# Grouped attention layer: scores and exponentials passed on in halves of 512 columns, small remainders moved between VectorE and GpSimd

## The chip, the cores and the metric

One core of one Trainium2 chip runs the whole program. The metric is the device time of one execution in microseconds (us), the median of several runs. A TensorE instruction is called a matmul; VectorE is DVE in the rows, ScalarE is ACT, GpSimd is POOL, SyncE (which here only starts transfers) is SP, and PEld is TensorE's load of the stationary operand.

## The reference

Four cross-attention layers are applied one after the other to x (4 batches, 512 tokens, 256 channels) against one context (4 batches, 1024 keys, 512 channels). Layers 0, 2 and 3 have 16 heads of 64 channels:

```python
q, k, v = x @ Wq, ctx @ Wk, ctx @ Wv                  # 16 heads x 64
logits = q @ k.T * 64 ** -0.5 + col_bias              # -20 at a few keys, by mask
x = softmax(logits) @ v @ Wo + bo + x
```

Layer 1 is the grouped one: 16 query heads of 16 channels share 4 key and value heads, and x is normalized first:

```python
xn = rmsnorm(x) * norm_w
q, k, v = xn @ wq, ctx @ wk, ctx @ wv                 # 16 q heads, 4 kv heads, each of 16
x = x + softmax(q @ k.T / 4) @ v @ wo
```

## The kernel before

The work is cut into 112 steps p, numbered through all layers. A wide step (layers 0, 2, 3) is one batch with two heads; a group step (p = 32 to 47, `G0` to `G1 - 1`) is one batch with four query heads of one group. A step passes through *slots*: in slot s the scores and exponentials of step s are made, the maxima of step s + 1, the projections of q and k for step s + 2, and the normalization and output projection of step s - 1. Each engine has its own queue, and its order is written out by hand: `wide_slot`, `turned_slot` and `group_slot` say, separately for TensorE, ScalarE and VectorE, what comes after what, and GpSimd has one loop over the slots. Nothing is reordered by a planner. The engines meet only at semaphores, each a counter that a finishing instruction raises and another engine waits for.

High precision comes from splitting: an f32 value is kept as an f16 high part (made by ScalarE or GpSimd) and an f16 low part, the remainder (made by VectorE or GpSimd), and a product is three f16 matmuls (`products`). `weights_lo` and `wo_lo` make the remainders of the projection weights and of the output weights, `context_lo` that of the context, `split_x_lo` that of x. In the group layer the weights change every four steps, at the end of slots 32, 36, 40 and 44. The weights for the next set are read into one buffer, `w_raw`; the load of the set after it (SP queue, `load_w`) waits until the remainder is made.

The inner pipeline of a group slot, which the change touches, has sixteen units of i. In each, TensorE does two matmuls of maxima for the next step (`maxima`, into `ps_st`), then the scores of a unit j (`group_scores`): two matmuls of 64 rows each, one per half h, into the two banks of `ps_sm`, 512 columns a bank. ScalarE turns both banks into `pt` with one exponential of 1024 columns (`exponentials`, L1473). There is only one `ps_sm`, so the scores of unit j + 1 wait for the exponential of unit j. After every second unit TensorE multiplies four `pt` pieces with the values (`group_attend`, L1039). VectorE reduces each unit's maxima (L1893). Slot 47, the last of the group layer, is different: its maxima are only eight and four more units follow.

At the start (slots -2 and -1) the context is split: ScalarE makes the high parts `context_hi(0..7)`, the low parts are made by VectorE (0, 1, 3) and GpSimd (2, 4 to 7); the low part of x of batches 0 and 1 is made by GpSimd. TensorE's first projection of q (`project_q`) waits for the low part of x.

Of the kernel before, what the change touches and what calls it, by code (L numbers as in the profile page):

```python
# [53 lines left out]
def layer_of(p):  # L54
    return max(n for n in range(LAYERS) if p >= STARTS[n])


def grouped(p):
    return G0 <= p < G1
# [304 lines left out]
def build(nc, a, out):  # L364
    with ExitStack() as ctx:
# [3 lines left out]
        def sem(name):  # L369
            return ctx.enter_context(nc.semaphore(name))  # L370
# [78 lines left out]
        s_wo_l = sem("s_wo_l")  # L449
        s_init = sem("s_init")  # L450
# [24 lines left out]
        s_exp = sem("s_exp")  # L475
        s_acc = sem("s_acc")
# [189 lines left out]
        def _(pool):  # L666
# [31 lines left out]

            def normed_lo(b):
                pool.wait_ge(s_xn_h, b + 1)  # L700
                pool.wait_ge(s_q, queries(G0 - B + b + 1))
                G.tensor_tensor(of_batch(xl, b), sq[:], of_batch(xh, b), ALU.subtract).then_inc(s_xs, 1)
# [64 lines left out]
            for s in range(-2, N - 1):  # L767
                now, far, past = 0 <= s < N, 0 <= s + 2 < N, 0 <= s - 1
                summing = now and not grouped(s)
                if s == -2:  # L770
                    pool.wait_ge(s_ext_k, 1)
                    split_x_lo(0, 0)
                    context_lo(2)
                elif s == -1:
                    split_x_lo(0, 1)
                    for n in range(4, 8):
                        context_lo(n)
                splitting = s >= 0 and far and layer_of(s + 2) != GROUPED and s + 2 - STARTS[layer_of(s + 2)] < B
# [28 lines left out]
                if grouped(s + 1) and has_values(s + 1):  # L807
                    column_of_ones(s + 1, 0)
                    column_of_ones(s + 1, 1)
            last_slot()  # L810

        @block.tensor
        def _(pe):
# [201 lines left out]
            def group_scores(p, j):  # L1015

                kt, tile, r = j // 2, j % 2, p % 3
                if p == G0 and j == 0:
                    pe.wait_ge(s_max, units(p + 1))
                else:  # L1020
                    pe.wait_ge(s_exp, units(p) + j)
                if j < 2:
                    pe.wait_ge(s_tile, 2 * groups(p) + 1 + tile)
                for h in range(2):
                    d = slice(h * HD, (h + 1) * HD)
                    last = MM(ps_sm[:, h, :], k_h[d, r, kt * P:(kt + 1) * P], queries_in(p, tile)[d, :], start=True,  # L1026
                              stop=True)
                last.then_inc(s_st, 1)
# [352 lines left out]
        def _(act):  # L1381
# [75 lines left out]
            def exponentials(p, j):  # L1457
                n = units(p) + j
                act.wait_ge(s_st, n + 1)
# [12 lines left out]
                src = ps_sm[:] if grouped(p) else ps_st[:, j % 2]  # L1472
                A(pt[:, n % RING, :], src.rearrange("p h q -> p (h q)"), ACT.Exp).then_inc(s_exp, 1)  # L1473
# [323 lines left out]
        def _(dve):  # L1797
# [20 lines left out]

            def weights_lo(w):
                r = w % 2  # L1820
                dve.wait_ge(s_w_h, w + 1)
                if layer_of_set(w) == GROUPED:
# [14 lines left out]
            def wo_lo(w):  # L1837
                dve.wait_ge(s_wo_h, w + 1)
                split_lo(wo_l[:], wo_raw[:], WS, wo_h[:]).then_inc(s_wo_l, 1)
# [131 lines left out]
            for step in range(5):  # L1971
                token_rows(0, step)
            context_lo(1)
# [5 lines left out]
            def wide_slot(s):  # L1979
# [29 lines left out]
                if s < 0:  # L2009
                    if s == -1:  # L2010
                        dve.wait_ge(s_ctx_l[1], 1)
                        context_lo(3)
                        keys_lo(s + 2, 0)
                    queries_lo(s + 2)
                elif far:
                    keys_lo(s + 2, 1)
# [66 lines left out]
            def group_slot(s):  # L2083
# [11 lines left out]
                for i in range(16):  # L2095
# [36 lines left out]
                    if i == 5 and (s - 1) % B == 0:  # L2132
                        wo_lo(set_of(s - 1))
# [6 lines left out]
                if s % B == 0:  # L2140
                    weights_lo(set_of(s) + 1)
# [111 lines left out]
```

## Time and profile before

| | us |
|---|---|
| Median of 3 runs (3498.06 to 3499.04) | 3498.78 |
| The profiled execution, time | 3498.58 |
| The profiled execution, span from first to last instruction | 3496.4 |
| TensorE busy | 3364.5 (96%) |
| VectorE busy | 2350.3 (67%) |
| GpSimd busy | 2183.0 (62%) |
| ScalarE busy | 1766.3 (51%) |

The span is the stretch from the first to the last recorded instruction; 2.2 us of the execution's time lie around it. Busy time is the union of an engine's instructions, so that a busy TensorE may still wait between two matmuls whose recorded ends overlap. The mean granted clock of TensorE is 0.993 of full speed.

### The profile page before, as it was taken

To read this page: it belongs to the slowest core of one execution; us is meant where nothing else is said; L and a number is where in the kernel's file an instruction comes from. 1 tells how busy PE (TensorE), PEld (TensorE's weight loads), DVE (VectorE), ACT (ScalarE), POOL (GpSimd) and SP (SyncE) were. 2 spreads that over 40 slices of the span, in tenths; PEclk is the share of its full clock that TensorE was granted. 3 is DMA by queue.
4 is the path that set the end of the run, shared out by engine and by line. 5 is a ranking of instruction groups with operands and counts; after the bars stand their busy time and mean duration, and the time that the engine had idled before them with its cause. 6 is when DMAs were issued, how large, how long until landed. Compare 5 with 4: busy or idle time off the path is not lost.

```text
span 3496.4 us, 70163 instructions
## 1 busy us (share of the span) xinstructions
PE 3364.5 (96%) x27442; PEld 1544.6 (44%) x27442; DVE 2350.3 (67%) x4444; ACT 1766.3 (51%) x2230; POOL 2183.0 (62%) x1050
## 2 busy tenths in 40 slices
PE   6999999999997888889999999999999999999998
PEld 3444444444442322234444444444444444444443
DVE  5666666666656788856676666666666666666666
ACT  4444444444445677764444444444444444444444
POOL 4877777777650000028777777777787677767776
PEclk8999999999999999999999999999999999999999
DMA  4000000000000000000000000000000000000000
GB/s 145 10 10 10 1 10 10 9 3 9 6 10 11 8 12 17 17 1 10 10 1 10 10 10 1 10 10 9 3 10 10 1 10 10 10 1 10 3 1 25
DMA packets 50178, 42.10 MB, mean 12 GB/s; under 512 B 4928, under 2 KB 42176, under 8 KB 49856
## 3 DMA queue, kind: packets, MB, share of 16 engines
q1 hardware_dynamic: 49136, 37.08, 3.5%
q8 instruction: 225, 3.69, 0.4%
q14 instruction: 97, 0.79, 0.1%
q10 hardware_dynamic: 720, 0.53, 0.1%
HBM read 32.36 MB, written 2.10 MB: 10 GB/s over the span
## 4 chain that ended last, share of the span: by engine, by line
PE 90%; ACT 3%; DVE 3%; POOL 2%; issue 2%; DMA 0%; SPq 0%; ACTq 0%; POOLq 0%; DVEq 0%
PE ps_j L863 39%; PE ps_j L1052 19%; PE ps_st L1012 13%; PE ps_sm L946 6%; PE ps_st L997 3%; PE ps_j L1039 3%; ACT pt L1473 2%; PE ps_sm L1026 2%; POOL acc L719 2%; PE ps_j L1072 1%; PE ps_st L946 1%; PE ps_j L955 1%; PE ps_j L1088 0%; PE ps_j L1063 0%; DVE nmg L1893 0%
## 5 line engine op out<-in xcount | busy, mean ns | idle before, releaser
L719 POOL TENSOR_TENSOR acc<-acc,pt 128x1024 f32<-128x1024 f32 x570 | 1365.3, 2395 | 438.9 <-ACT pt L1473 384.8
L1473 ACT ACTIVATE pt<-ps_st 128x1024 f32<-128x1024 f32 x768 | 743.0, 1019 | 447.0 <-PE ps_st L1012 435.2
L1052 PE MATMUL ps_j<-pt,v 128*64 128x512 f32 x3040 | 694.2, 598 | 1.4 <-DVE q_l L1808 1.3
L1903 DVE CUSTOM_DVE_ANT_0 ps_sm<-ps_sm,bias_m,nmx 128x512 f32<-128x512 f32 x666 | 480.3, 757 | 272.6 <-PE ps_j L946 227.6
L863 PE MATMUL ps_j<-w_h,ctx_h 128*128 128x128 f16 x3072 | 532.6, 220 | 1.6 <-ACT rinv L1489 1.1
L863 PE MATMUL ps_j<-w_l,ctx_h 128*128 128x128 f16 x3072 | 531.5, 219 | 0.0
L863 PE MATMUL ps_j<-w_h,ctx_l 128*128 128x128 f16 x3072 | 531.4, 219 | 0.0
L1903 DVE CUSTOM_DVE_ANT_0 ps_sm<-ps_sm,bias_m 128x512 f32<-128x512 f32 x486 | 334.5, 706 | 197.1 <-PE ps_j L946 186.4
L740 POOL TENSOR_TENSOR o_un<-o_un,rinv 128x512 f32<-128x512 f32 x111 | 142.0, 1280 | 477.2 <-ACT rinv L1485 294.9
L1052 PEld LDWEIGHTS ps_j<-pt,v 128*64 128x64 f32 x3040 | 201.7, 136 | 407.6 <-issue 369.6
L1940 DVE RECIPROCAL rinv<-rinv 128x256 f32<-128x256 f32 x190 | 331.3, 1746 | 14.0 <-ACT rinv L1489 4.5
L1893 DVE TENSOR_REDUCE nmg<-ps_st 128x2 f32<-128x1024 f32 x248 | 296.0, 1217 | 45.7 <-PE ps_st L946 44.5
L863 PEld LDWEIGHTS ps_j<-w_h,ctx_h 128*128 128x128 f16 x3072 | 301.1, 98 | 54.9 <-issue 40.6
L863 PE MATMUL ps_j<-ctx_h,w_h 128*128 128x512 f16 x800 | 304.9, 381 | 15.5 <-DVE w_l L1808 13.1
L1473 ACT ACTIVATE pt<-ps_sm 128x1024 f32<-128x1024 f32 x256 | 261.6, 1022 | 104.7 <-PE ps_sm L1026 104.6
L946 PE MATMUL ps_sm<-k_h,q_h 64*128 64x512 f16 x1160 | 294.1, 381 | 14.3 <-DVE nmx L1903 11.6
L863 PEld LDWEIGHTS ps_j<-w_l,ctx_h 128*128 128x128 f16 x3072 | 301.4, 98 | 10.7
L863 PE MATMUL ps_j<-ctx_l,w_h 128*128 128x512 f16 x800 | 304.4, 381 | 0.0
L863 PE MATMUL ps_j<-ctx_h,w_l 128*128 128x512 f16 x800 | 304.2, 380 | 0.0
L863 PEld LDWEIGHTS ps_j<-w_h,ctx_l 128*128 128x128 f16 x3072 | 301.4, 98 | 0.0
L1433 ACT ACTIVATE k_h<-ps_j 128x512 f16<-128x512 f32 x192 | 114.6, 597 | 366.9 <-PE ps_j L863 366.9
L1012 PE MATMUL ps_st<-q_h,k_h 64*128 64x512 f16 x1488 | 282.4, 376 | 0.0
(186 smaller groups left out, 5483.0 us busy)
## 6 DMA issues: line engine op xcount, KB each, us to landing
w_raw<-wk SPq DMA_DIRECT2D x25, 256.0 KB, 2.7
pt<-ctx_t SPq DMA_DIRECT2D x6, 1024.0 KB, 7.8
w_raw<-wv SPq DMA_DIRECT2D x24, 256.0 KB, 3.7
wo_raw<-wo SPq DMA_DIRECT2D x28, 128.0 KB, 2.0
w_raw<-wq SPq DMA_DIRECT2D x24, 128.0 KB, 2.8
k_h<-k_l SPq DMA_DIRECT2D x72, 32.0 KB, 1.9
x<-x_t SPq DMA_DIRECT2D x4, 512.0 KB, 8.9
acc<-ctx_t SPq DMA_DIRECT2D x2, 1024.0 KB, 8.1
```

What stands on the lines that cost most here:

```text
L719: G.tensor_tensor(total, first, pt[:, n % RING, :], ALU.add).then_inc(s_acc, 1)
L740: G.tensor_tensor(o, o, rinv[:], ALU.mult).then_inc(s_o, 1)
L863: done = MM(dst, l, r, start=first and i == 0, stop=last and i == n - 1)
L946: last = MM(dst[h], queries_in(p, tile)[d, t * P:(t + 1) * P], k_h[d, r, half * HALF:(half + 1) * HALF], start=True, stop=True)
L997: MM(ps_st[:, j % 2, j // 2, :], ext_k[rows, buf, kt * P:(kt + 1) * P], ext_q[rows, p % 2, :], start=True, stop=False)
L1012: last = MM(ps_st[:, side, h, :], k[d, r, keys], q[d, r, :], start=False, stop=n == 2)
L1052: last = MM(dst[h * HD:(h + 1) * HD, :], values_of(p)[:, kt, h * HD:(h + 1) * HD], pt[:, (units(p) + kt) % RING, h * TQ:(h + 1) * TQ], sta ...
L1433: A(k_h[:, r, keys], bank(f"k{half}", p), ACT.Copy, scale=1 / WS).then_inc(s_k_h, 1)
L1473: A(pt[:, n % RING, :], src.rearrange("p h q -> p (h q)"), ACT.Exp).then_inc(s_exp, 1)
L1893: V.tensor_reduce(nmg[:, half, t, 2 * tile:2 * tile + 2], maxima_in(p, u), AX_X, ALU.max, negate=True).then_inc(s_max, 1)
L1903: last = V.tensor_tensor_reduce(out=src, in0=src, in1=bias_m[:, t, half * HALF:(half + 1) * HALF], scale=-1.0, scalar=nmx[:, 0, t, h:h + 1 ...
L1940: V.reciprocal(r, r).then_inc(s_rinv, 1)
```

## The change

In the group layer a unit's scores and exponential are passed on one bank at a time. `group_scores` waits for the first half of the previous exponential (`s_exp_first`), issues the matmul of half 0, then waits for the second half (`s_exp`), and issues the matmul of half 1; each of the two matmuls raises a semaphore of its own. `exponentials` becomes two activations of 512 columns, each of which waits for its own matmul.

The rests (the low parts) are dealt out differently. In the group layer GpSimd makes the low parts of the weights and of the output weights, at the end of slots 32, 36, 40 and 44; VectorE no longer does. [...] At the start VectorE makes the low part of x of batches 0 and 1, and GpSimd makes the context's low part 3, after waiting for the end of VectorE's mask preparation (`s_init`).

```diff
+            def weights_lo(w):                 # GpSimd
+                r = w % 2
+                pool.wait_ge(s_w_h, w + 1)
+                pool.wait_ge(s_w_l, w)
+                if layer_of_set(w) == GROUPED:
+                    cols = slice(WQ0, WQ0 + CQ * 2 * P)
+                    for c in range(CQ):
+                        cc = slice(WQ0 + c * 2 * P, WQ0 + (c + 1) * 2 * P)
+                        G.tensor_scalar(w_raw[:, cc], w_raw[:, cc], norm_w[:, c:c + 1], None, ALU.mult).then_inc(s_w_s, 1)
+                else:
+                    cols = slice(0, WCOLS)
+                    G.tensor_scalar(w_raw[:], w_raw[:], WS, None, ALU.mult).then_inc(s_w_s, CQ)
+                pool.wait_ge(s_w_s, CQ * (w - G0 // B))
+                G.tensor_tensor(w_l[:, r, cols], w_raw[:, cols], w_h[:, r, cols], ALU.subtract).then_inc(s_w_l, 1)
...
                 if s == -2:
-                    pool.wait_ge(s_ext_k, 1)
-                    split_x_lo(0, 0)
+                    pool.wait_ge(s_init, 1)
                     context_lo(2)
+                    context_lo(3)
                 elif s == -1:
-                    split_x_lo(0, 1)
                     for n in range(4, 8):
                         context_lo(n)
+                elif s == 0:
+                    pool.wait_ge(s_xs, 2)
...
+                if grouped(s) and s % B == 0:
+                    weights_lo(set_of(s) + 1)
+                    wo_lo(set_of(s))
...
-                    pe.wait_ge(s_exp, units(p) + j)
+                    pe.wait_ge(s_exp_first, units(p) - units(G0) + j)
...
-                    last = MM(ps_sm[:, h, :], k_h[d, r, kt * P:(kt + 1) * P], queries_in(p, tile)[d, :], start=True,
-                              stop=True)
-                last.then_inc(s_st, 1)
+                    if h and (p != G0 or j):
+                        pe.wait_ge(s_exp, units(p) + j)
+                    MM(ps_sm[:, h, :], k_h[d, r, kt * P:(kt + 1) * P], queries_in(p, tile)[d, :], start=True, stop=True
+                       ).then_inc(s_st if h else s_st_first, 1)
...
-                src = ps_sm[:] if grouped(p) else ps_st[:, j % 2]
-                A(pt[:, n % RING, :], src.rearrange("p h q -> p (h q)"), ACT.Exp).then_inc(s_exp, 1)
+                if grouped(p):
+                    A(pt[:, n % RING, 0:TQ], ps_sm[:, 0], ACT.Exp).then_inc(s_exp_first, 1)
+                    act.wait_ge(s_st, n + 1)
+                    A(pt[:, n % RING, TQ:2 * TQ], ps_sm[:, 1], ACT.Exp).then_inc(s_exp, 1)
+                    return
...
             split_x_lo(b):                     # VectorE, once after token_rows(0, ...), once in slot -1
+                dve.wait_ge(s_xs_h, b + 1)
+                V.tensor_tensor(of_batch(xl, b), of_batch(x32, b), of_batch(xh, b), ALU.subtract).then_inc(s_xs, 1)
...
                     if s == -1:
-                        dve.wait_ge(s_ctx_l[1], 1)
-                        context_lo(3)
+                        split_x_lo(1)
                         keys_lo(s + 2, 0)
...
-                    if i == 5 and (s - 1) % B == 0:
-                        wo_lo(set_of(s - 1))
...
-                if s % B == 0:
-                    weights_lo(set_of(s) + 1)
```

The instructions of TensorE keep their places; what differs are their waits. TensorE at the end of one unit of a group slot and in the next one (L946 are the maxima, L1026 the scores, L1039 the multiplication with the values), before:

```order
L1026 MATMUL ps_sm<-q_l,k_h 128x512 [waits s_tile,s_exp]
L1026 MATMUL ps_sm<-q_l,k_h 128x512
L946 MATMUL ps_st<-k_h,q_h 128x512 [waits s_max,s_q_l,s_kb]
L946 MATMUL ps_st<-k_h,q_h 128x512
```

and the same place in the change, where L1060 are the scores and L978 the maxima:

```order
L1060 MATMUL ps_sm<-q_l,k_h 128x512 [waits s_tile,s_exp_first]
L1060 MATMUL ps_sm<-q_l,k_h 128x512 [waits s_exp]
L978 MATMUL ps_st<-k_h,q_h 128x512 [waits s_max,s_q_l,s_kb]
L978 MATMUL ps_st<-k_h,q_h 128x512
L1060 MATMUL ps_sm<-q_h,k_h 128x512 [waits s_exp_first]
L1060 MATMUL ps_sm<-q_h,k_h 128x512 [waits s_exp]
L1072 MATMUL ps_j<-pt,v 32x512 [waits s_ones,s_exp]
```

The second matmul of a unit, which waited for nothing of its own, now waits for the second exponential; everything behind it on the queue stands behind that wait, as it stood behind the first matmul's wait before.

GpSimd at the very start, before (L680 is the low part of x, L696 that of the context, L676 the high part of x of slot 0):

```order
L680 TENSOR_TENSOR xl<-x,xh 128x2x512
L696 TENSOR_TENSOR ctx_l<-pt,ctx_h 128x4x512
L680 TENSOR_TENSOR xl<-x,xh 128x2x512
L696 TENSOR_TENSOR ctx_l<-pt,ctx_h 128x4x512 x3
L696 TENSOR_TENSOR ctx_l<-acc,ctx_h 128x4x512
L676 TENSOR_SCALAR xh<-x 128x2x512
```

and in the change:

```order
L700 TENSOR_TENSOR ctx_l<-pt,ctx_h 128x4x512
L700 TENSOR_TENSOR ctx_l<-acc,ctx_h 128x4x512
L700 TENSOR_TENSOR ctx_l<-pt,ctx_h 128x4x512 x3
L700 TENSOR_TENSOR ctx_l<-acc,ctx_h 128x4x512
L680 TENSOR_SCALAR xh<-x 128x2x512
```

Both parts of x have left this queue and one part of the context (3, from the buffer `acc`) has come in, so that five long instructions of one kind stand in a row.

VectorE in slot -1, between the fourth and the fifth maximum of step 0, before (L1816 is the context's low part 3, L1808 the low parts of k and q):

```order
L1903 ISA nmx 128x1
L1816 TENSOR_TENSOR ctx_l<-acc,ctx_h 128x4x512
L1808 SCALAR_TENSOR_TENSOR k_l<-ps_j,k_h 128x512
L1808 SCALAR_TENSOR_TENSOR q_l<-ps_j,q_h 128x512
L1903 ISA ps_sm,nmx<-ps_sm,bias_m,nmx 128x512
```

and in the change:

```order
L1951 ISA nmx 128x1
L1861 TENSOR_TENSOR xl<-x,xh 128x2x512
L1848 SCALAR_TENSOR_TENSOR k_l<-ps_j,k_h 128x512
L1848 SCALAR_TENSOR_TENSOR q_l<-ps_j,q_h 128x512
L1951 ISA ps_sm,nmx<-ps_sm,bias_m,nmx 128x512
```

The place stays the same, the instruction in it is half as long in elements, and is now one that TensorE's projection of q waits for.

## Rows read from the trace of the kernel before

**Rows 1.** The page's part on busy time: engine, us, share, instructions.
```profile
PE 3364.5 (96%) x27442; PEld 1544.6 (44%) x27442; DVE 2350.3 (67%) x4444; ACT 1766.3 (51%) x2230; POOL 2183.0 (62%) x1050
```

**Rows 2.** Busy time by stretch: us of each engine, instructions, PE clock, DMA.
```profile
800.00:900.00 100.00, 100.00 (x852) 47.90 (x850) 65.10 (x137) 47.52 (x62) 71.21 (x34) 1.00 0.03 8
...
1240.00:1280.00 40.00, 35.77 (x246) 11.38 (x246) 33.07 (x35) 28.92 (x33) 2.43 (x2) 0.96 0.06 14
```

**Rows 3.** Groups of instructions, 1036 to 1566 us: total, mean ns, idle before.
```profile
L1473 ACT ACTIVATE pt<-ps_sm 128x1024 f32<-128x1024 f32 x256 | 261.6, 1022 | 104.7 <-PE ps_sm L1026 104.6
...
L745 POOL TENSOR_TENSOR o_l<-o_un,o_h 128x512 f16<-128x512 f32 x16 | 18.5, 1158 | 71.0 <-ACT o_h L1524 71.0
...
L676 POOL TENSOR_SCALAR xh<-x 128x1024 f16<-128x1024 f32 x3 | 8.3, 2776 | 16.6 <-DVE x L1948 16.6
```

**Rows 4.** Who waited for whom, 1036 to 1566 us: total us, times, longest.
```profile
ACT pt L1473 <- PE ps_sm L1026: 104.6, 142, 6.3
...
PEld ps_sm L1026 <- ACT pt L1473: 70.8, 85, 3.6
...
POOL o_un L740 <- ACT rinv L1485: 294.9, 15, 24.1
```

**Rows 5.** Timeline in group slots 38 and 39: start us, us, engine, line, [idle before].
```profile
1289.40 1.02 ACT L1473 ACTIVATE pt<-ps_sm 128x1024 f32<-128x1024 f32 x1
...
1290.47 0.39 PE L1026 MATMUL ps_sm<-q_l,k_h 64*128 64x512 f16 x2
...
1294.41 0.38 PE L1026 MATMUL ps_sm<-q_l,k_h 64*128 64x512 f16 x2
...
1294.84 1.02 ACT L1473 ACTIVATE pt<-ps_sm 128x1024 f32<-128x1024 f32 x1 [0.46 <-PE ps_sm L1026]
...
1295.91 0.39 PE L1026 MATMUL ps_sm<-q_h,k_h 64*128 64x512 f16 x2 [0.91 <-ACT pt L1473]
...
1296.23 1.06 PE L1039 MATMUL ps_j<-pt,acc 128*32 128x512 f32 x8
```

**Rows 6.** Timeline of ACT, two 512-column copies in a row.
```profile
40.32 1.08 ACT L1553 ACTIVATE bias_m<-ps_j 128x512 f16<-128x512 f32 x2
```

**Rows 7.** Timeline of PE in a wide slot.
```profile
306.00 0.38 PE L946 MATMUL ps_sm<-k_h,q_h 64*128 64x512 f16 x2
...
306.30 3.65 PE L1052 MATMUL ps_j<-pt,v 128*64 128x512 f32 x16
```

**Rows 8.** Timeline of the last group slot, 47.
```profile
1555.28 0.39 PE L1026 MATMUL ps_sm<-q_l,k_h 64*128 64x512 f16 x2
...
1556.79 0.39 PE L1026 MATMUL ps_sm<-q_h,k_h 64*128 64x512 f16 x2 [0.37 <-ACT pt L1473]
```

**Rows 9.** Timeline of the first 50 us, DVE, POOL, PE and ACT.
```profile
17.94 2.29 DVE L1816 TENSOR_TENSOR ctx_l<-pt,ctx_h 128x2048 f16<-128x2048 f32 x1
...
17.98 4.22 POOL L680 TENSOR_TENSOR xl<-x,xh 128x1024 f16<-128x1024 f32 x1 [17.56 <-DVE ext_k L1865]
...
20.15 2.34 DVE L1974 TENSOR_SCALAR sq<-sq 128x512 f32<-128x512 f32 x1
...
40.50 4.07 POOL L696 TENSOR_TENSOR ctx_l<-pt,ctx_h 128x2048 f16<-128x2048 f32 x1 [5.50 <-ACT ctx_h L1394]
...
41.69 5.03 DVE L1816 TENSOR_TENSOR ctx_l<-acc,ctx_h 128x2048 f16<-128x2048 f32 x1
...
43.65 0.38 PE L863 MATMUL ps_j<-xh,w_h 128*128 128x512 f16 x1
...
45.14 0.60 ACT L1442 ACTIVATE q_h<-ps_j 128x512 f16<-128x512 f32 x1 [0.70 <-PE ps_j L863]
...
47.84 0.74 DVE L1903 CUSTOM_DVE_ANT_0 ps_sm<-ps_sm,bias_m,nmx 128x512 f32<-128x512 f32 x1
```

**Rows 10.** Timeline of the slot after a change of weights.
```profile
1237.28 0.42 ACT L1423 ACTIVATE wo_h<-wo_raw 128x256 f16<-128x256 f32 x1 [1.64 <-PE ps_j L863]
...
1240.84 1.66 PE L1039 MATMUL ps_j<-pt,v 128*32 128x512 f32 x8
```

More of the change, by code:

```diff
@@ L449, in build @@
         s_wo_l = sem("s_wo_l")
+        s_w_s = sem("s_w_s")
+        s_wo_s = sem("s_wo_s")
         s_init = sem("s_init")
@@ L475, in build @@
         s_exp = sem("s_exp")
+        s_st_first = sem("s_st_first")
+        s_exp_first = sem("s_exp_first")
         s_acc = sem("s_acc")
@@ L697, in context_lo, with wo_lo @@
                                 ALU.subtract).then_inc(s_ctx_l[n // 2], 1)
+            def weights_lo(w):
[12 more added lines that the diff above has]
+                G.tensor_tensor(w_l[:, r, cols], w_raw[:, cols], w_h[:, r, cols], ALU.subtract).then_inc(s_w_l, 1)
+            def wo_lo(w):
+                pool.wait_ge(s_wo_h, w + 1)
+                pool.wait_ge(s_wo_l, w)
+                G.tensor_scalar(wo_raw[:], wo_raw[:], WS, None, ALU.mult).then_inc(s_wo_s, 1)
+                pool.wait_ge(s_wo_s, w - G0 // B + 1)
+                pool.wait_ge(s_out, 2 * B * w)
+                G.tensor_tensor(wo_l[:], wo_raw[:], wo_h[:], ALU.subtract).then_inc(s_wo_l, 1)
             def normed_lo(b):
@@ L1458, in exponentials @@
                 n = units(p) + j
-                act.wait_ge(s_st, n + 1)
+                if grouped(p):
+                    act.wait_ge(s_st_first, n - units(G0) + 1)
+                else:
+                    act.wait_ge(s_st, n + 1)
                 if n >= RING:
@@ L1471, in exponentials @@
                     act.wait_ge(s_ctx_l[(STAGES + n // 2) // 2], (STAGES + n // 2) % 2 + 1)
-                src = ps_sm[:] if grouped(p) else ps_st[:, j % 2]
-                A(pt[:, n % RING, :], src.rearrange("p h q -> p (h q)"), ACT.Exp).then_inc(s_exp, 1)
+                if grouped(p):
+                    A(pt[:, n % RING, 0:TQ], ps_sm[:, 0], ACT.Exp).then_inc(s_exp_first, 1)
+                    act.wait_ge(s_st, n + 1)
+                    A(pt[:, n % RING, TQ:2 * TQ], ps_sm[:, 1], ACT.Exp).then_inc(s_exp, 1)
+                    return
+                A(pt[:, n % RING, :], ps_st[:, j % 2].rearrange("p h q -> p (h q)"), ACT.Exp).then_inc(s_exp, 1)
             def sums_hi(p):
@@ L1817, in context_lo, with split_x_lo @@
                                 ALU.subtract).then_inc(s_ctx_l[n // 2], 1)
+            def split_x_lo(b):
+                dve.wait_ge(s_xs_h, b + 1)
+                V.tensor_tensor(of_batch(xl, b), of_batch(x32, b), of_batch(xh, b), ALU.subtract).then_inc(s_xs, 1)
             def weights_lo(w):
@@ L1821, in weights_lo @@
                 dve.wait_ge(s_w_h, w + 1)
+                if w == G1 // B + 1:
+                    dve.wait_ge(s_w_l, w)
                 if layer_of_set(w) == GROUPED:
@@ L1838, in wo_lo @@
                 dve.wait_ge(s_wo_h, w + 1)
+                if w == G1 // B:
+                    dve.wait_ge(s_wo_l, w)
                 split_lo(wo_l[:], wo_raw[:], WS, wo_h[:]).then_inc(s_wo_l, 1)
@@ L1972, in _ @@
                 token_rows(0, step)
+            split_x_lo(0)
             context_lo(1)
```

## The prediction, made before the change was run

> **What bounds the kernel now.** I read the page first: TensorE is busy for 96% of the span [rows 1]. Then busy time by stretch, since such a share is a mean over stages. In a wide stretch TensorE has no gap at all, 100.00 of 100 us; in the group layer it has 35.77 of 40, and no other engine is full: VectorE 33.07, ScalarE 28.92, GpSimd 2.43 [rows 2]. So in the wide layers, 96 of 112 steps, only less TensorE work would help, and the change takes none away. It can act in two places: the group layer, about 1036 to 1566 us, and the start, where the context is split.
>
> Third, the waits of the group layer. ScalarE waits 142 times for scores, 104.6 us, and TensorE's weight load for scores waits 85 times for an exponential, 70.8 us [rows 4]. Each sees the other as late: a loop. Scores (0.39 us), a step of 0.05, exponential 1.02 us, a step of 0.05, next scores: 1.51 us, as 1290.47 and the scores after it show, and 1555.28 to 1556.79 once more [rows 5, 8].
>
> Fourth, the timeline of a slot, to see which end of the loop decides. At 1294.41 the scores of an odd unit start, TensorE having been free for them; at 1294.84 their exponential, for 1.02 us; at 1295.91 the next scores, 0.05 after its end, and only then, at 1296.23, the multiplication of 1.06 us [rows 5]. During that long multiplication the next exponential runs hidden. So TensorE meets a finished exponential at odd units and an unfinished one at even units, and there it waits for an exponential whose scores it had issued without delay.
>
> **The change part by part. The halves.** The new order lets scores of half 0 start when the first 512 columns are read out, about half an exponential earlier. But the next matmul, of half 1, waits for the second half, and TensorE's queue is in order: maxima, multiplication and projections stand behind it. What TensorE waits for is therefore still the end of the whole exponential j, and the exponential starts when its own scores are done, as before. In the 1294 case: both score matmuls issue at 1294.41 side by side, the first half starts at 1294.84 at the latest, and the second half ends after two activations of 512 columns. Two such reads of PSUM in a row take 1.08 us [rows 6], one exponential of 1024 takes 1.02 [rows 3]. TensorE is released 0.06 later, not earlier. The first half may start some 0.01 to 0.02 earlier, since it waits for one matmul only; bounds per unit therefore 0.04 to 0.06, I take 0.06, because a second semaphore is in the path.
>
> How often it counts: in an ordinary slot the scores start within 0.06 us of an exponential's end seven times of sixteen. Five are in the wait view (85 over 16 slots [rows 4]); in two the gap is too small to be an idle entry, such as 1290.47, where the exponential ends at 1290.42 [rows 5]. 16 x 7 = 112 times 0.06 is +6.7 us; by the 85 alone and 0.04 it is +3.4. In the other nine units TensorE comes later than the exponential's end by 0.09 or more, and that margin covers most of the 0.06; I add nothing.
>
> What it gives back: where two waits follow each other with nothing long between, as at 1555.28 and 1556.79 in slot 47 [rows 8], the early half 0 does help. The second exponential can then start as soon as the first ends; the loop of 1.51 becomes ScalarE's 1.08, -0.4 each. In an ordinary slot the multiplication breaks every such run. I count three, in slots 33 and 47: -1.2. At 1290.47 the maxima end with the exponential, so that TensorE itself couldn't come earlier: 0.
>
> The pair of score matmuls must still run side by side despite the wait between them. A wide slot has such a pair: the closing maxima at 306.00 have a wait for a semaphore (`s_max_a`) between the two halves, and the next instruction starts 0.30 later [rows 7], against 0.32 for the pair of scores at 1295.91 [rows 5]. Cost 0; the bound from above is one more matmul, 0.21, if they came one after the other.
>
> Half 0 now also raises a semaphore. The Trainium skill (TensorE: Matmul & The Clock Gate, The cost: per-tile semaphore tail) says that increments on packed tiles are written one after the other, about 26 ns each, and advises one on the last. By that rule each of the 112 waits grows by another 0.026, +2.9 us. No row here separates it, and the sum doesn't use it.
>
> Sum for the halves: 6.7 - 1.2 = +5.5 us.
>
> **Weights' rests to GpSimd, group layer.** VectorE loses a little work four times. It isn't waited for there: it has 6.9 of 40 us to spare [rows 2]. After a change of weights what delays the first exponential is ScalarE's wait of 1.64 us for the output projection ahead of `wo_hi` [rows 10], and that stays. Gain 0. GpSimd gets two scalings of 256 columns, a subtraction of 512, then 256 and 256. By 2.776 us for a scaling of 1024 and 1.158 for a subtraction of 512 [rows 3] that is 0.7 + 0.7 + 1.2 + 0.7 + 0.6 = 3.9 us; for the wide set 3.5 + 2.9 + 1.3 = 7.7. GpSimd is idle for 294.9 us over 15 waits, some 20 a slot [rows 4], and it is the normalization queued behind it that ends this idle time: covered. The next load of weights waits for it too, but by the order of the code it is used only a set later. Without cover it would cost 3 x 3.9 + 7.7 = 19 us.
>
> **The start.** Here the rows show a mechanism that decides: GpSimd and VectorE exclude each other on some instructions. GpSimd's part of x takes 4.22 us at 17.98, while VectorE works on the context for 2.29; VectorE's scaling `sq` takes 2.34 at 20.15, and ends with GpSimd's; VectorE's context part takes 5.03 at 41.69, ending 2.15 after GpSimd's own of 40.50 [rows 9]. The Trainium skill (SBUF — State Buffer, Who interferes with whom) has it as an exclusive lock on a shared pair of ports, taken for a whole instruction when VectorE has two SBUF inputs; the trace agrees, 5.03 against 2.29.
> At first the change gains. x of batch 0 on VectorE costs half of 2.29, 1.2 us, ahead of the context part; GpSimd waits then, so `sq` falls from 2.34 to about 0.45. Everything behind is 0.7 earlier.
> In slot -1 the gain is lost. x of batch 1 stands on VectorE at 41.69 - 0.7 = 41.0, but GpSimd holds the ports from 40.50 - 0.7 = 39.8 to 43.9. It ends at 43.9 + 1.2 = 45.1. The projection of q, which started at 43.65, waits for exactly this; its high part followed 1.49 later and took 0.60, and the low part is another pass of some 0.7 over 512 columns, like the maximum's 0.74: 45.2 + 1.5 + 0.6 + 0.7 = 48.0 for the next maximum, against 47.84 [rows 9]. Before, the same maximum waited for VectorE's long context part. One wait replaces another: 0. Bounds: -2.1 if the lock misses it (the projection then starts at 43.65 - 0.7 = 42.95, and the maximum is at 45.75), +1.5 if TensorE, idle longer before the second half of k, runs that at 1.2 GHz.
>
> Total: 3498.58 + 5.5 + 0 + 0 = 3504.1; the profiled execution is 0.2 below the median of the runs, so that I say 3504.
>
> **The rivals.** A, faster, on the other side: the halves shorten the loop wherever it is waited for. Each of the 85 waits would lose the 0.43 from scores to exponential less 0.06; with half of them so, 43 x 0.37 = -16, 3483. For it: 104.6 us of ScalarE waiting for scores. Against: the exponential waited for belongs to scores that were not late; it decides once the projections don't fill the odd units.
> B, the start gains its 2.1 and the halves cost as said: 3502. Against: GpSimd has 1.2 us of lead.
> C, slower: TensorE's clock. In the slot after a change of weights the granted clock is 0.96 over 40 us [rows 2], and the multiplication takes 1.66 us, against 1.06 in others [rows 10, 5]: some matmuls run at 1.2 instead of 2.4 GHz, after ScalarE has kept TensorE waiting. If the longer waits bring that into the other 12 slots, at about 1 us a slot, it is 12 + 5.5: 3516. Against: the waits grow by 0.06 only, and half 0 now works inside them.
> D, slower: the pair no longer overlaps, 0.21 in the 144 units where TensorE isn't waiting: +30, 3534. Against: rows 7.
> E, the change does nothing measurable: the 0.06 is hidden by margins; 3498.6.
>
> **How the numbers follow.** A change of under 0.2%, 7.0 us, can't be told from none. Chances: forecast 0.55 (own range 3501 to 3508), A 0.10, B 0.12, C 0.13, D 0.04, E 0.06. Of the forecast's 0.55 some 0.16 lie above 3505.8, and 0.02, gains of the clock with it, below 3491.8. Of A all but 0.01 is faster; C and D are slower; B and E are the same. Slower: 0.16 + 0.13 + 0.04 = 0.33. Faster: 0.02 + 0.09 = 0.11. Same: 0.37 + 0.01 + 0.12 + 0.06 = 0.56. The range 3492 to 3516 leaves out D, most of A and the edge of C.
>
> **What would show it.** The halves: two activations of 0.60 in 1.08 us; scores of half 1 at 0.05 after the second; TensorE's waits for exponentials in an ordinary slot as many as now, each 0.05 to 0.06 longer; an ordinary slot 0.4 longer; half 0 of the scores alone inside the wait. GpSimd: its new instructions at about 1236 to 1240 us with nobody waiting. The start: VectorE's x of batch 1 over 3 us long, and the maximum of 47.84 within 1 us of its place. The prediction is wrong if waits at even units shrink, if VectorE's x of batch 1 takes 1.2, or if multiplications of 1.7 us appear in most slots.

## The result, and the profile of the changed kernel

The change takes 3503.91 us (median of 20 runs, 3502.47 to 3505.29) against 3498.86 (20 runs, 3497.53 to 3499.47): ratio 1.0015, 95% interval 1.0008 to 1.0021. It is slower by 5.05 us, 0.14%; the forecast was 3504. The profiled execution took 3503.15 with a span of 3501.4, 5.0 longer than before's 3496.4. So the total came out as said. The split did not: the prediction had all of it in the group layer, and the trace has half of it ahead of it. (One of the eleven runs with two exponentials, further down, took 4180.72 us at a mean granted clock of 0.781; it counts in that kernel's median and not in its ratio.)

The page of the change on busy time, as in [rows 1]:

```profile
PE 3388.0 (97%) x27442; PEld 1548.8 (44%) x27442; DVE 2344.5 (67%) x4434; ACT 1779.5 (51%) x2486; POOL 2200.3 (63%) x1068
```

TensorE is busy for 23.5 us more with the same number of instructions. That is no more work. Half 0 of the scores now starts inside a wait and half 1 behind it, and the stretch between counts as busy: the pair at 1299.89 below is one entry of 0.87 us, where it was 0.39 [rows 5]. Busy time by stretch, the second of [rows 2]:

```profile
1240.00:1280.00 40.00, 35.90 (x229) 10.50 (x229) 32.26 (x34) 29.58 (x55) 6.37 (x7) 0.96 0.08 21
```

TensorE's share is as before (35.77), and GpSimd's 6.37 instead of 2.43 are its new rests. Its groups, with those of the exponentials, from 1036 to 1566 us (the columns are those of [rows 3]):

```profile
L1509 ACT ACTIVATE pt<-ps_sm 128x512 f32<-128x512 f32 x254 | 151.1, 595 | 83.3 <-PE ps_sm L1060 83.3
...
L712 POOL TENSOR_SCALAR w_raw<-w_raw,norm_w_sb 128x256 f32<-128x256 f32 x6 | 5.5, 924 | 18.3 <-ACT w_h L1441 18.3
```

The waits there, as in [rows 4]:

```profile
POOL o_un L768 <- ACT rinv L1525: 266.5, 15, 22.5
ACT pt L1509 <- PE ps_sm L1060: 83.3, 112, 6.2
PEld ps_sm L1060 <- ACT pt L1509: 36.9, 43, 3.2
PEld ps_sm L1060 <- ACT pt L1511: 34.6, 106, 0.4
```

TensorE's one wait of a unit has become two: for the first exponential and then, at most 0.4 us, for the second. Together they are 71.5 us, where [rows 4] had 70.8. The second wait shows 106 times over the layer's 16 slots, nearly seven a slot. In the timeline, in the same slot as [rows 5]:

```profile
1294.87 0.45 PE L1060 MATMUL ps_sm<-q_l,k_h 64*128 64x512 f16 x2
...
1298.60 0.39 PE L978 MATMUL ps_st<-k_h,q_l 64*128 64x512 f16 x2
1298.82 0.38 PE L1060 MATMUL ps_sm<-q_l,k_h 64*128 64x512 f16 x2
1299.04 0.38 PE L978 MATMUL ps_st<-k_h,q_h 64*128 64x512 f16 x2
1299.23 0.60 ACT L1509 ACTIVATE pt<-ps_sm 128x512 f32<-128x512 f32 x1 [0.56 <-PE ps_sm L1060]
1299.73 0.59 ACT L1511 ACTIVATE pt<-ps_sm 128x512 f32<-128x512 f32 x1
1299.89 0.87 PE L1060 MATMUL ps_sm<-q_h,k_h 64*128 64x512 f16 x2 [0.47 <-ACT pt L1509]
...
1300.69 1.07 PE L1072 MATMUL ps_j<-pt,acc 128*32 128x512 f32 x8
```

From the scores to the multiplication behind the next scores it is 1300.69 - 1298.82 = 1.87 us, and was 1296.23 - 1294.41 = 1.82 [rows 5]. The two activations take 1299.73 + 0.59 - 1299.23 = 1.09. The pair at 1294.87 is one whose twin before, at 1290.47, had a gap too small for an idle entry [rows 5]: it now takes 0.45 and not 0.39, because half 1 waits for the second exponential.

Where the 5 us arise is seen best at a mark that comes once a slot. VectorE's short reduction `nmx<-nmg` closes each slot's maxima. Before:

```profile
1056.31 0.19 DVE L1912 TENSOR_REDUCE nmx<-nmg 128x16 f32<-128x32 f32 x1
...
1292.52 0.19 DVE L1912 TENSOR_REDUCE nmx<-nmg 128x16 f32<-128x32 f32 x1
...
1320.21 0.19 DVE L1912 TENSOR_REDUCE nmx<-nmg 128x16 f32<-128x32 f32 x1
...
1524.74 0.19 DVE L1912 TENSOR_REDUCE nmx<-nmg 128x16 f32<-128x32 f32 x1
```

and in the change:

```profile
1058.65 0.19 DVE L1960 TENSOR_REDUCE nmx<-nmg 128x16 f32<-128x32 f32 x1
...
1296.92 0.19 DVE L1960 TENSOR_REDUCE nmx<-nmg 128x16 f32<-128x32 f32 x1
...
1324.87 0.19 DVE L1960 TENSOR_REDUCE nmx<-nmg 128x16 f32<-128x32 f32 x1
...
1529.72 0.19 DVE L1960 TENSOR_REDUCE nmx<-nmg 128x16 f32<-128x32 f32 x1
```

The first mark is 2.34 us later, so that in these two executions this much was lost before the group layer (how far such a mark moves by itself is seen in the experiments). The last is 4.98 later, 2.64 more. An ordinary slot takes 27.95 (1296.92 to 1324.87), and took 27.69 (1292.52 to 1320.21): 0.26 more, not 0.42.

The start, as in [rows 9]:

```profile
17.60 1.23 DVE L1861 TENSOR_TENSOR xl<-x,xh 128x1024 f16<-128x1024 f32 x1
...
20.94 0.42 DVE L2023 TENSOR_SCALAR sq<-sq 128x512 f32<-128x512 f32 x1
...
24.28 0.38 PE L895 MATMUL ps_j<-ctx_h,w_h 128*128 128x512 f16 x1 [3.86 <-DVE k_l L1848]
...
41.86 4.06 POOL L700 TENSOR_TENSOR ctx_l<-pt,ctx_h 128x2048 f16<-128x2048 f32 x1 [6.67 <-ACT ctx_h L1427]
...
42.80 0.63 PE L895 MATMUL ps_j<-ctx_l,w_h 128*128 128x512 f16 x1
...
43.05 3.95 DVE L1861 TENSOR_TENSOR xl<-x,xh 128x1024 f16<-128x1024 f32 x1
...
46.42 0.38 PE L895 MATMUL ps_j<-ctx_h,w_l 128*128 128x512 f16 x1
...
47.10 0.38 PE L895 MATMUL ps_j<-xh,w_h 128*128 128x512 f16 x1 [0.30 <-issue]
...
49.83 0.75 DVE L1951 CUSTOM_DVE_ANT_0 ps_sm<-ps_sm,bias_m,nmx 128x512 f32<-128x512 f32 x1
```

and of before, the first matmul of k for step 1 and that of the second half of k in slot -1:

```profile
25.41 0.58 PE L863 MATMUL ps_j<-ctx_h,w_h 128*128 128x512 f16 x1 [0.34 <-DVE k_l L1808]
...
41.06 0.38 PE L863 MATMUL ps_j<-ctx_h,w_h 128*128 128x512 f16 x1 [0.36 <-ACT bias_m L1553]
```

The early half is as forecast: x of batch 0 takes 1.23, `sq` fell from 2.34 to 0.42. So is the lock: x of batch 1 on VectorE takes 3.95, ending 1.1 behind GpSimd's context part. The projection of q begins 0.1 after it, at 47.10. But the maximum that was to come at 48.0 comes at 49.83, 1.99 later than before.

### The profile page after: what moved, and what is told of

Its sections match the earlier page's. It is cut to its first block, busy times and chain, and to the rows that moved or that the text cites. A ratio compares the mean times of both kernels' runs of the same rounds, so it can differ in the third digit from the quotient of the medians.

```text
span 3501.4 us, 70441 instructions
## 1 busy us (share of the span) xinstructions
PE 3388.0 (97%) x27442; PEld 1548.8 (44%) x27442; DVE 2344.5 (67%) x4434; ACT 1779.5 (51%) x2486; POOL 2200.3 (63%) x1068
## 4 chain that ended last, share of the span: by engine, by line
PE 90%; ACT 2%; DVE 2%; POOL 2%; issue 2%; DMA 0%; SPq 0%; ACTq 0%; POOLq 0%; DVEq 0%
PE ps_j L895 39%; PE ps_j L1085 19%; PE ps_st L1044 13%; PE ps_sm L978 6%; PE ps_j L1072 3%; PE ps_st L1029 3%; PE ps_sm L1060 2%; POOL acc L747 2%; PE ps_st L978 2%; PE ps_j L1105 1%; PE ps_j L987 1%; ACT pt L1511 1%; PE ps_j L1121 0%; PE ps_j L1096 0%; DVE nmg L1941 0%
## 5 line engine op out<-in xcount | busy, mean ns | idle before, releaser
L768 POOL TENSOR_TENSOR o_un<-o_un,rinv 128x512 f32<-128x512 f32 x111 | 141.6, 1276 | 450.0 <-ACT rinv L1525 266.5
L978 PE MATMUL ps_sm<-k_h,q_h 64*128 64x512 f16 x1160 | 294.1, 381 | 15.0 <-DVE nmx L1951 12.3
L1044 PE MATMUL ps_st<-q_h,k_l 64*128 64x512 f16 x1488 | 282.4, 376 | 0.0
```

The lines of the kernel that those rows point to most:

```text
L768: G.tensor_tensor(o, o, rinv[:], ALU.mult).then_inc(s_o, 1)
L978: last = MM(dst[h], queries_in(p, tile)[d, t * P:(t + 1) * P], k_h[d, r, half * HALF:(half + 1) * HALF], start=True, stop=True)
L1044: last = MM(ps_st[:, side, h, :], k[d, r, keys], q[d, r, :], start=False, stop=n == 2)
```

## The experiments

Each was timed beside the kernel before, in 11 runs (4 for four exponentials); the medians stand together first.

| kernel | us | against before, 95% |
|---|---|---|
| halves alone | 3502.41 | 1.0011 (1.0002 to 1.0019) |
| two exponentials, scores unchanged | 3503.00 | 1.0014 (1.0005 to 1.0023) |
| four exponentials, scores unchanged | 3527.43 | 1.0082 (1.0068 to 1.0096) |
| rests of the group layer alone | 3498.58 | 0.9999 (0.9990 to 1.0008) |
| start alone | 3500.49 | 1.0005 (0.9996 to 1.0014) |
| start, no lock | 3499.27 | 1.0003 (0.9994 to 1.0012) |
| start, x of batch 1 early | 3498.53 | 1.0001 (0.9992 to 1.0010) |
| start, q held back | 3501.40 | 1.0006 (0.9997 to 1.0015) |
| start, both | 3498.21 | 0.9997 (0.9988 to 1.0006) |
| halves, half 0 ahead in every second unit | 3492.42 | 0.9985 (0.9976 to 0.9994) |
| the same in every unit | 3495.06 | 0.9989 (0.9980 to 0.9998) |
| whole change, mended | 3494.20 | 0.9987 (0.9978 to 0.9996) |

The kernel before had medians of 3498.92, 3498.69, 3498.95 and 3498.92 in the four sets. The halves, the start and the rests add up: 3.5 + 1.6 - 0.3 = 4.8, against the change's 5.05. Where two intervals overlap, as those of the five kernels of the start do, the order of their medians is not shown clear of noise.

**Halves alone.** Of the change's diff the parts in `group_scores` and `exponentials`.

> Only the handing over by banks in the group layer; rests and start as before. Theory 1 (the split of the loss read from the two traces: half of the 5.0 us arises in the group layer): +2.6 us against the kernel before, the mark of the last group slot 2.6 later, the first mark at its old place within 0.2. Theory 2 (the prediction's sum): +5.5. Theory 3 (the group layer's loss comes from the weights' rests on GpSimd, or from the start's clock, and not from the halves): within 0.5 of the kernel before.

+3.5 us, between theories 1 and 2. Its marks tell why the trace had less:

```profile
1055.34 0.18 DVE L1922 TENSOR_REDUCE nmx<-nmg 128x16 f32<-128x32 f32 x1
...
1527.26 0.19 DVE L1922 TENSOR_REDUCE nmx<-nmg 128x16 f32<-128x32 f32 x1
```

The ordinary slot between them is again 27.95. From first to last mark it is 471.92, 3.49 more than before's 468.43. The change's own is 471.07. The difference lies in the three slots after a change of weights, where a stretch at the lower clock falls now longer, now shorter: together they took 91.30 before, 91.69 here and 90.78 in the change. It also shows what one trace can't tell: this kernel's start is that of before, and its first mark lies 0.97 us earlier. Seven of the kernels traced here have the start of before, and their first marks lie between 1055.33 and 1057.61, 2.28 us apart. The change's 1058.65 is behind all of them, but how much of the 2.34 is the change's cannot be read from two traces.

**Two exponentials, then four.** TensorE's part is left as it was; ScalarE makes two activations of 512 columns, or four of 256, and raises one semaphore.

```diff
+                if grouped(p):
+                    A(pt[:, n % RING, 0:TQ], ps_sm[:, 0], ACT.Exp)
+                    A(pt[:, n % RING, TQ:2 * TQ], ps_sm[:, 1], ACT.Exp).then_inc(s_exp, 1)
+                    return
...
```

> Only ScalarE's part of the halves: two exponentials of 512 columns in a row, one semaphore after the second; TensorE's scores wait for both and are issued side by side as before. Theory 1 (the loss is the longer read of PSUM, 0.05 to 0.06 us in each of five waits of an ordinary slot, and the early half 0 gives nothing back): +3.5 us, as the handing over by banks alone measured (3502.41 against 3498.92), within 0.7. Theory 2 (the second semaphore, or the wait between the two matmuls, makes the loss): about 0. Theory 3 (the early half 0 hides a part of the longer read): above +4.5.

> As the run with two exponentials, with four of 256 columns each, to see how the loss grows with the number of pieces. Two pieces make the whole 0.06 us longer (1.08 against 1.02), so four should make it about 0.18 longer. Theory 1 (the loss is that length times the five waits of a slot, plus more waits once the margin of 0.09 in two other units is used up): +10 to +16 us. Theory 2 (the loss has to do with the semaphores): no more than the run with two exponentials.

Two pieces cost +4.3 us, between theory 1's upper end (4.2) and theory 3's 4.5: the loss is there without the second semaphore and without the wait inside the pair (theory 2 falls). Four cost +28.7, nearly twice the upper end. An ordinary slot, from mark to mark, is 28.04 with two (1297.51 to 1325.55), 0.09 more than with the handing over (27.95); the four other slots of this kind agree within 0.01, though the profiled execution was one of 3507.42 us, 4.4 above the median. So the handing over does give a little back in ordinary slots: over some 14 slots 1.2 us, of which the medians show 0.8 (4.3 against 3.5), within their intervals. This run differs from the halves in the early half 0, in the second semaphore and in the wait inside the pair, so that 0.09 is what all three leave together. With four it is 29.17 (1305.82 to 1334.99), and the timeline shows the reason:

```profile
1314.89 0.39 PE L1026 MATMUL ps_sm<-q_l,k_h 64*128 64x512 f16 x2
1315.33 1.21 ACT L1475 ACTIVATE pt<-ps_sm 128x256 f32<-128x256 f32 x4 [0.49 <-PE ps_sm L1026]
...
1316.59 0.39 PE L1026 MATMUL ps_sm<-q_h,k_h 64*128 64x512 f16 x2 [1.00 <-ACT pt L1475]
```

The whole exponential takes 1.21, 0.19 more than 1.02, as worked out. What was wrong is the count: one round of scores and exponential is now 1.70 us (1314.89 to 1316.59), and a slot loses 1.48, nearly eight times 0.19 and not five times. By the timeline seven units of a slot wait already with the halves (see the account of the prediction below), and with four pieces some that had a margin join them.

**Rests alone.** The change's `weights_lo` and `wo_lo` on GpSimd, group layer only.

> Only the group layer's weight rests on GpSimd. Theory 1 (covered by GpSimd's idle time of some 20 us a slot, nobody waits): 0 within 0.5 us. Theory 2 (VectorE's relief lets the slot after a change of weights come earlier, in which the trace after the change saved 0.7 us once): -0.7 to -3. Theory 3 (GpSimd's rests delay its normalization): up to +19.

-0.3 us, within theory 1. From first to last mark it is 468.44 us, as before (468.43).

**The start, five ways.** First the change's start alone; then x of batch 1 moved on VectorE from behind the fourth maximum of slot -1 to behind the second; then back at its place, but with GpSimd's context part 4 waiting for it; then the first projection of q held back; then early and held.

```diff
                 peak()
                 peak()
+                if s == -1:
+                    split_x_lo(1)
...
-                        split_x_lo(1)
```

```diff
                 elif s == -1:
+                    pool.wait_ge(s_xs, 2)
                     for n in range(4, 8):
                         context_lo(n)
```

```diff
+                    else:
+                        pe.wait_ge(s_init, 1)
                     project_q(s + 2, 0)
```

> Only the start dealt out anew: x on VectorE, the context's low part 3 on GpSimd. Theory 1 (the traces: the first group mark is 2.3 us later and this arises before 50 us): +2.3 us, with the projection of k of slot -1, second half, at the lower clock (about 4.4 us long where it was 2.6). Theory 2 (the prediction's value): 0, with -2.1 to +1.5 as bounds.

> The start dealt out anew, but VectorE makes x of batch 1 after the second maximum of slot -1, where it idles, instead of after the fourth, where GpSimd's context part 4 blocks it. Theory lock (the loss of the start is VectorE's wait of 3.95 us, which the projection of q waits for): the loss of 2.3 goes and up to 2 us are gained against the kernel with the start alone. Theory clock (TensorE idles after its first projection of q and then runs k's projections at 1.2 GHz; those ended at 46.8, only 0.25 us before x of batch 1 was ready at 47.0): at most 0.3 to 0.5 us better than the start alone, so +1.8 to +2.0 against the kernel before.

> The start dealt out anew as in the change, the low part of x of batch 1 at the same place on VectorE, but GpSimd's context part 4 waits for it, so that both aren't at work at once. Theory lock (the start loses because that instruction takes 3.96 us instead of 1.2 while GpSimd has the ports): it takes 1.2 again, and the loss of the start alone (+1.6) goes: 3497 to 3499. Theory place (x of batch 1 is simply late, whatever its length): still +1.6. GpSimd's part 4 is then about 1.3 us later, which would cost only if the second half of k of step 2 waits for it.

> The start dealt out anew, and TensorE's first projection of q waits for the end of the mask preparation, some 4 us more, so that TensorE idles before it and not behind it, as in the kernel before. Theory clock (the start loses because TensorE runs v and k at 1.2 GHz for longer after its idle time now lies behind q): the loss of the start alone (+1.6 us) goes, 0 within 0.5. Theory lock (VectorE's x of batch 1, blocked for 3.95 us instead of 1.2, is what costs): still +1.6 within 0.5.

> Both: x of batch 1 early in slot -1 on VectorE, and the first projection of q held back. Theory lock (the early x alone measured -0.4 against the kernel before and -2.0 against the start alone): -0.4 within 0.5. Theory clock, on top of it: about -2, since each removes a loss of its own.

The start alone measured +1.6 us, between its two theories. The interval of its ratio takes in zero, but ten of its eleven runs lie above the slowest of the 33 of before beside them, and the sum of the parts needs it. Theory clock fell three times by the medians: x early recovers 2.0 us where it allowed 0.5; with q held back the second half of k does run at 2.4 GHz, and yet the time is +2.7; and with both it is -0.5, where it wanted -2 and theory lock -0.4. (The run with q held back is no clean test and misses theory lock's 1.6 within 0.5 too: holding q also makes the second half of k start at 43.57.) Without the lock, at the same place, the median is 3499.27, +0.3, just above theory lock's 3497 to 3499:

```profile
42.83 1.22 DVE L1823 TENSOR_TENSOR xl<-x,xh 128x1024 f16<-128x1024 f32 x1
...
46.12 0.38 PE L865 MATMUL ps_j<-ctx_h,w_l 128*128 128x512 f16 x1
46.34 0.38 PE L865 MATMUL ps_j<-xh,w_h 128*128 128x512 f16 x1
...
49.07 0.75 DVE L1909 CUSTOM_DVE_ANT_0 ps_sm<-ps_sm,bias_m,nmx 128x512 f32<-128x512 f32 x1
```

x takes 1.22 again, and q's projection begins 0.22 after k's last matmul (46.12, 46.34), where the change needs 0.68 (46.42, 47.10).

What the lock costs is seen once traces of one kind are compared. With the start of before there are two kinds. In four traces (before, rests, four exponentials, every unit) the granted clock from 43 to 45 us is 1.00, all twelve matmuls of the second half of k run at 2.4 GHz, and the maximum comes at 47.44 to 47.84. In three (halves, two exponentials, every second unit) it is 0.50, eight of the twelve run at 1.2 GHz, and the maximum comes at 48.72 to 48.91; the halves alone:

```profile
43.17 0.63 PE L865 MATMUL ps_j<-ctx_l,w_h 128*128 128x512 f16 x1
...
48.89 0.75 DVE L1913 CUSTOM_DVE_ANT_0 ps_sm<-ps_sm,bias_m,nmx 128x512 f32<-128x512 f32 x1
```

The change's trace is of the second kind (0.50) and was set beside one of the first, so that about 1 us of its 1.99 is a difference that also stands between two executions with the same start. Against the second kind the change (49.83) and the start alone (49.66) are 0.75 to 1.1 late, the run without the lock (49.07) 0.2 to 0.4, and x early (48.05) is 0.7 to 0.9 ahead: at the maximum the lock costs 0.6.

That the whole 1.2 us between the medians of the start alone and the run without the lock arises in the start is not shown. The profiled executions differ by 1.0 in their spans (3498.3, 3497.3): the first marks by 0.37 (1058.31, 1057.94), the group layer by 2.33, in its three slots after a change of weights, and behind the last mark the run without the lock is 1.70 slower; from 3455 to 3480 us, in a wide layer, its granted clock is 0.93 and that of the start alone 1.00. Of the 1.9 us that x early gains in the traces, 1.36 stand at the first mark.

**Half 0 ahead of the maxima.** The early half gives so little because behind the multiplication TensorE issues both halves together, late (1298.82 above). In this version every second unit issues half 0, the two maxima (upper rows first), half 1, so that neighbours still use different rows.

```diff
+            def one_unit(m, u, p, j):
+                if j % 2 == 0:
+                    maxima(m, u)
+                    group_scores(p, j)
+                    return
+                group_scores(p, j, (0,))
+                maxima(m, u, True)
+                group_scores(p, j, (1,))
...
```

> Halves handed over as in the change (start and rests as before), but in every second unit, the one behind the multiplication with the values, TensorE issues half 0 of the scores first, then the unit's two maxima (half 1, half 0), then half 1 of the scores. Theory 1 (the early half gives nothing back in the change because TensorE issues both halves together right behind the multiplication; the wait that counts is one exponential after that): the first exponential starts 0.22 us earlier, the five waits of an ordinary slot shrink by 0.22 each from the halves' 27.95, so 26.9 us a slot, and about -15 us against the halves alone (3502.4), 3487. Theory 2 (the scores no longer run side by side with each other and each pair costs 0.21 more): +0.21 in up to 8 units of a slot, 3502 to 3530. Theory 3 (what TensorE waits for is not moved by the order): 3502 within 1.

> As the run with every second unit, in every unit. In the unit in which TensorE waits, half 0 is then issued as soon as the first exponential of 512 columns is done, and the maxima follow it. Theory 1: as there, 3487, since the end of this wait is still the second exponential; within 1 us of it. Theory 2 (VectorE gets its maxima later and TensorE begins to wait for it): 3 us or more above it.

3492.42, 6.5 us faster than the kernel before and 10.0 than the halves alone, between theories 1 and 3. An ordinary slot is 27.31:

```profile
1288.31 0.19 DVE L1936 TENSOR_REDUCE nmx<-nmg 128x16 f32<-128x32 f32 x1
...
1315.62 0.19 DVE L1936 TENSOR_REDUCE nmx<-nmg 128x16 f32<-128x32 f32 x1
```

```profile
1289.98 0.39 PE L1041 MATMUL ps_sm<-q_l,k_h 64*128 64x512 f16 x1
1289.99 0.60 PE L948 MATMUL ps_st<-k_h,q_l 64*128 64x512 f16 x2
1290.21 0.38 PE L1041 MATMUL ps_sm<-q_l,k_h 64*128 64x512 f16 x1
1290.41 0.60 ACT L1493 ACTIVATE pt<-ps_sm 128x512 f32<-128x512 f32 x1 [0.35 <-PE ps_sm L1041]
1290.42 0.38 PE L948 MATMUL ps_st<-k_h,q_h 64*128 64x512 f16 x2
...
1295.07 1.07 PE L1053 MATMUL ps_j<-pt,acc 128*32 128x512 f32 x8
...
1297.95 1.06 PE L1053 MATMUL ps_j<-pt,acc 128*32 128x512 f32 x8
```

and the same two multiplications in the change:

```profile
1304.11 1.07 PE L1072 MATMUL ps_j<-pt,acc 128*32 128x512 f32 x8
...
1307.21 1.06 PE L1072 MATMUL ps_j<-pt,acc 128*32 128x512 f32 x8
```

Half 0 issues at 1289.98, half 1 at 1290.21, and the next maxima at 1290.42: the four matmuls take 0.44 us, as two pairs do (1298.60 to 1299.04 in the change), and theory 2 falls. The exponential starts 0.43 after half 0. The gain is 0.64 a slot and not 1.1, because it comes at three places and not at five. Of the eight stretches from one multiplication with the values to the next that follow a mark, the second, third and last are shorter by 0.21, 0.22 and 0.19 (the third is shown, 2.88 against 3.10); the others take what they took. Why those do not shrink was not tested. The same in every unit is 2.6 us slower by medians, between its two theories. VectorE's waits for maxima grew only from 50.3 to 55.5 us, and ordinary slots by no more than 0.08. In the profiled runs 2.3 us of it lie in the three slots after a change of weights (91.75 against 89.46), where the clock plays in, so that the cause stays open.

**The whole change, mended.** The new order, x of batch 1 early, GpSimd's rests.

> The whole change with its two losses mended: the halves with half 0 issued ahead of the maxima in every second unit, and x of batch 1 early in slot -1 on VectorE; the group layer's rests on GpSimd. Theory 1 (the parts add up: -6.5 for the halves in that order, -0.4 for the start with x early, -0.3 for the rests, each as measured alone against the kernel before): 3491.7, within 1 us, with the first mark of the group layer at about 1057 and ordinary slots of 27.3. Theory 2 (the parts collide, as GpSimd's weights' rests or the early x take something from the new order): 3494 or more.

3494.20, 4.7 us faster than before and 9.7 faster than the change, but 2.5 above the sum of its parts, which was theory 2's figure. Its ordinary slots are 27.31 as expected and the first mark is at 1055.53. Its runs spread from 3488.99 to 3500.36, and in the profiled one the three slots after a change of weights took 92.3, against 89.5 in the run of the new order alone. So the parts do not collide in the ordinary slots. Whether GpSimd's rests or only the clock makes those three longer is open. Of all versions timed, the new order alone has the lowest median, but its interval (0.9976 to 0.9994) and that of the mended change (0.9978 to 0.9996) overlap.

## Why the prediction came out right, and where it was wrong

- **What bounds it**: right. From the last mark to the end it is 1971.7 us before and after (3496.4 - 1524.74, 3501.4 - 1529.72); the differences arose in the start and the group layer.
- **Price of a wait in the halves**: right, 0.05 where I took 0.06. 1.87 against 1.82 in the timeline is 0.05, two activations took 1.09. With one semaphore, in the run with two exponentials, a slot lost more (28.04), not less.
- **Number of waits**: right, seven a slot; the sum of 0.42 a slot was still too high. In the slot from 1296.92 on, half 1 stands 0.06 or 0.07 behind the end of a second exponential in exactly the seven units that I had counted, the two with a gap too small for an entry among them. They are the pairs at 1299.89, 1303.56, 1306.40, 1311.74, 1319.28, 1322.82 and 1324.18, which take 0.87, 0.62, 0.87, 0.68, 0.45, 0.45 and 0.58 us; the two of 0.45 are those without an entry before, as the one shown at 1294.87 in the slot ahead. At six of the seven the scores fall behind those of before by another 0.05, 0.05, 0.04, 0.07, 0.06 and 0.05, together 0.32. At the seventh they gain 0.01, and 0.05 come back in the unit behind it: 0.26. My lower figure of +3.4, five waits by 0.04, came close to the measured +3.5 by luck: it had too few waits and no gain.
- **What the early half gives back**: this is the term that was mis-sized. I had put it at 0 in ordinary slots and at 0.4 in each of three runs. In an ordinary slot it is 0.09 against the run with two exponentials and some 0.11 by the timeline: behind the pair at 1294.87, where half 0 starts 0.06 ahead of half 1, no multiplication stands but a short projection, and the next wait is shorter by as much. In slot 47 the gain is 0.14 and not 0.4 [rows 8]:

```profile
1559.12 1.06 PE L1072 MATMUL ps_j<-pt,acc 128*32 128x512 f32 x8
...
1560.12 0.56 PE L1060 MATMUL ps_sm<-q_l,k_h 64*128 64x512 f16 x2
...
1562.00 1.06 PE L1072 MATMUL ps_j<-pt,acc 128*32 128x512 f32 x8
```

  From multiplication to multiplication it is 2.88 now and was 3.02 (1554.09 to 1557.11): TensorE comes to the scores only at 1560.12, because the multiplication ahead of them takes an us, so that half 0 is only 0.17 ahead of half 1 (the pair takes 0.56, not 0.39).
- **The pair stays side by side**: right, 0.38 for both at 1298.82, and 0.45 at 1294.87 with the wait of 0.06 inside it. Rival D is out.
- **The Trainium skill's price of a second increment** (TensorE: Matmul & The Clock Gate, The cost: per-tile semaphore tail), +2.9 us, is not to be seen here: with two increments a slot of seven waits lost 0.26 us, and with one, in the run with two exponentials, 0.35. No run changed the increments alone.
- **Rests of the group layer**: right, -0.3 measured. GpSimd's part for one change of weights takes two scalings of 0.92, 1.15, 0.85 and 0.67, 4.5 us and not 3.9, and for the wide set 3.44, 2.61, 0.85 and 0.67, 7.6 as forecast (7.7); its waits for the normalization fell from 294.9 to 266.5 and covered them.
- **The start**: wrong by 1.6 us by the median, past my bound of +1.5. The lock came exactly as said, 3.95 long. The step that failed is "everything behind is 0.7 earlier". TensorE did begin the first half of k for step 1 1.1 us earlier (24.28 for 25.41), but seven of its twelve matmuls ran at 1.2 GHz (0.63 us each, and 0.38 at 2.4 GHz), so that VectorE's gain was gone. In the seven traces with the start of before at most two of these twelve did; with the new start and q not held back it was seven or eight in four of five (in the mended change none). The second half of k then began at 42.42 and not at 40.4, x of batch 1 at 43.05 and not at 41.0, and behind it everything took what I had said. Against before's 41.06 that is 1.4 late, of which 0.7 to 0.9 is the difference between the two kinds of trace with the old start (41.06 there, 41.72 to 41.91 in the slow ones). I then read the clock as the whole cause, and the runs took that back: by the medians, 1.2 of the 1.6 us are gone without the lock. How the rest is shared between the lock and the clock stays open.
- **Rivals**: B (the start gains 2.1) lost its sign; A is what the change did not do but could: with half 0 ahead of the maxima the loop does shorten, by 6.5 us in the end, not 16. C did not show: ordinary slots are all 27.95 or 27.37 within 0.01, without multiplications of 1.7.

That the total was right within 0.1 us is luck: two errors of opposite sign, 2.0 too much for the halves and 1.6 too little for the start, nearly cancel.

## What to carry to other kernels

Cutting a result into halves to hand it over earlier pays only if the consumer's queue reaches the first half earlier too; look at what stands ahead of it, and interleave. Count a dependence that ends just in time as a wait, even where the wait view has no entry for it: what makes the awaited instruction longer costs there too. Where a slot has a mark that comes once, compare its first and last occurrence before believing a total. And before reading a difference of one or two us at the start from two traces, look how far traces of the same code lie apart.

## What the runs showed of the hardware

- The price of cutting an activation that reads PSUM: 1.02 us for 1024 columns in one, 1.09 in two, 1.21 in four.
- Four matmuls of 64 rows on alternating halves of the rows (scores, maxima, maxima, scores) ran as closely as two pairs, 0.44 us for all four.
- A VectorE subtraction of 1024 elements took 1.22 us alone and 3.95 beside GpSimd's of 2048, which had begun first and itself was not slowed (4.06, and 4.07 in the run without the lock).
- With the same code of the start, the granted clock from 43 to 45 us was 1.00 in four traces and 0.50 in three, and the first mark of the group layer moved by 2.28 us.
- TensorE's busy time rose by 23.5 us with no instruction more, since a matmul that waits inside a pair lets the pair count as busy.
